# Source rows of an edge loop: gathered from memory, or made on chip by products of transposed one-hots

## The reference

```python
h = jnp.maximum(_layernorm(x, axis=-1), 0.0)
row, col = (edge_index[0], edge_index[1])
m = jnp.concatenate([x[row], x[col]], axis=1)
m = jax.nn.relu(m @ Wm1 + bm1)
m = jax.nn.relu(m @ Wm2 + bm2)
m_sum = jax.ops.segment_sum(m, row, num_segments=x.shape[0])
```

## Time and profile before

| | us |
|---|---|
| median of 3 runs (lowest, highest) | 1143.71 (1141.4, 1145.15) |
| profiled execution | 1144.47 |
| its span, first to last instruction | 1142.0 |
| TensorE busy | 841.2 (74%) |
| weight loads busy | 533.9 (47%) |
| VectorE busy | 661.6 (58%) |
| ScalarE busy | 461.4 (40%) |
| GpSimd busy | 368.7 (32%) |
| mean granted clock of TensorE | 0.914 of full |

### The profile page before, as it was taken

One profiled execution on the slowest core, in us unless ns is written; L12 is line 12 of the kernel. 1 busy time (PEld: TensorE's weight loads), 2 busy tenths in 40 slices (PEclk: granted clock), 3 DMA queues, 4 the chain that ended last, 5 costly groups with the idle time before them and its releaser, 6 DMA issues.

```text
span 1142.0 us, 17135 instructions
## 1 busy us (share of the span) xinstructions
PE 841.2 (74%) x5085; PEld 533.9 (47%) x5086; DVE 661.6 (58%) x1761; ACT 461.4 (40%) x956; POOL 368.7 (32%) x472
## 2 busy tenths in 40 slices
PE   4999627867787867677777768777687868776447
PEld 2568416756665756566666654531123213211243
DVE  6499924444444444444535446379848885996551
ACT  5321005434444444444435446534454444454200
POOL 7000265445554555545454550011301320212000
PEclk9999959888898899998989999889989999999778
DMA  2210132222222222222222340000000000000300
GB/s 70 88 44 1 33 97 64 65 78 69 87 72 80 73 92 70 77 74 73 83 73 83 73 91 1 1 0 1 1 1 0 1 1 1 0 1 0 148 1 19
DMA packets 26801, 53.84 MB, mean 47 GB/s; under 512 B 7440, under 2 KB 14736, under 8 KB 26768
## 3 DMA queue, kind: packets, MB, share of 16 engines
q0 software_dynamic: 14208, 38.82, 12.0%
q1 hardware_dynamic: 12560, 14.63, 3.9%
HBM read 46.60 MB, written 6.82 MB: 47 GB/s over the span
## 4 chain that ended last, share of the span: by engine, by line
PE 39%; DVE 19%; another core or an unknown queue 16%; ACT 12%; issue 9%; POOL 3%; ACTq 1%; DVEq 1%; DMA 0%; POOLq 0%
DVE OHd L853 8%; PE PS L989 6%; ACT OHe L470 5%; DVE PS L864 4%; PE PS L1089 3%; PE PS L1205 3%; PE PS L1131 2%; PE PS L1042 2%; PE PS L1196 2%; PE PS L1166 2%; PE PS L1086 2%; ACT OHs L472 2%; PE PS L1099 1%; PE PS L1107 1%
## 5 line engine op out<-in xcount | busy, mean ns | idle before, releaser
L364 POOL DMA_INDIRECT BT<-Ptab,gidx x148 | 143.2, 967 | 286.2 <-DVE MS L758 190.4
L470 ACT ACTIVATE OHe<-OHs,sew 128x128 bf16<-128x128 bf16 x408 | 126.9, 390 | 91.0 <-PE PS L1042 49.4
L364 POOL DMA_INDIRECT BT<-Qtab,gidx x148 | 143.1, 967 | 45.1 <-issue 45.1
L853 DVE CUSTOM_DVE_ANT_0 OHd<-PS,n1T 128x1024 bf16<-128x1024 f32 x96 | 113.4, 1219 | 15.7 <-PE PS L1166 15.7
L795 DVE TENSOR_SCALAR OHd<-iotaN,dstf 128x1024 bf16<-128x1024 f16 x136 | 64.5, 516 | 99.6 <-PE PS L1042 57.2
L1086 PE MATMUL PS<-OHd,OHc 128*128 x284 | 64.2, 226 | 69.0 <-ACT OHs L472 65.4
L758 DVE TENSOR_TENSOR MS<-BT 128x512 f32 x68 | 47.1, 692 | 113.7 <-remote 108.5
L393 POOL TENSOR_TENSOR zl<-AL,Sx 128x8 f32<-128x8 f32 x12 | 11.4, 947 | 291.0 <-DVE Sx L853 291.0
L1196 PE MATMUL PS<-rowA,sel 128*128 128x512 bf16 x192 | 61.5, 407 | 47.1 <-DVE PS L864 38.5
L1099 PE MATMUL PS<-OHs,m2s 128*128 128x128 f32 x544 | 89.6, 317 | 0.0
L1036 PE MATMUL PS<-Wm,m1T 128*128 128x256 f32 x272 | 85.7, 398 | 0.0
(11 more groups left out here) (326 smaller groups left out, 1663.3 us busy)
## 6 DMA issues: line engine op xcount, KB each, us to landing
BT<-Wtab SPq DMA_DIRECT2D x1, 4096.0 KB, 13.0
BT<-Ptab,gidx POOLq DMA_INDIRECT x148
BT<-Qtab,gidx POOLq DMA_INDIRECT x148
Wtab<-H SPq DMA_DIRECT2D x4, 512.0 KB, 2.7
Wtab<-cs SPq DMA_DIRECT2D x4, 512.0 KB, 3.2
Ptab<-BT SPq DMA_DIRECT2D x1, 1024.0 KB, 4.6
Qtab<-BT SPq DMA_DIRECT2D x1, 1024.0 KB, 7.1
Wn<-in_L_gnn_Wn SPq DMA_DIRECT2D x1, 1024.0 KB, 5.4
```

The costliest lines, as they stand in the source:

```text
L364: g.indirect_dma_start(out=G[:, p % SLOTS, t, k, :], out_offset=None, in_=tab, in_offset=bass.IndirectOffsetOnAxis(ap=gidx[:, p, 2 * t + k ...
L470: a.activation(OHe[:, k, j, :], OHs[:, k, :], ACT.Copy, scale=sew[:, j, bass.ds(2 * g + k, 1)])
L853: v.tensor_tensor_reduce(junk[n % 2], bank(4, 2), mask[:, i, :], 1.0, 2 * FAR, ALU.subtract, ALU.max, Sx[:, i, hd:hd + 1]).then_inc(S("gat ...
```

## The change

- The rows of P are no longer stored and gathered. GpSimd splits P into three bf16 parts (`Pp`, in the room of SKT, which is used later), L371 to L377 of the new file; the three add up to P. In the loop TensorE multiplies, for each chunk of a pair, a one-hot of the edge's source, transposed (nodes on partitions, edges on columns), with the three parts of the source block: six products of 256 columns into bank 5 (`sources`).
- The transposed one-hot is made by GpSimd (`turned`): it compares a row of source numbers, which stands on all partitions (`srow`), with the partition's number. The row comes from a transposition of `srcl` on TensorE, a copy to bytes on ScalarE, a store to memory (Stab) and two loads that spread it over all partitions: the first 8 pairs' part, then the rest.
- The message is bank 5 plus the gathered Q rows. A number for a pair's block is packed into the word that TensorE loads for each pair (`pblk`, `span`).
- The bias bm2 is added by VectorE from PSUM into m2s, and ScalarE's relu then works in place; the two bias products and the bf16 parts of bm2 go.
- The ranks move from bank 5 to the second half of bank 4, so five banks are cleared, and the rank products for the next pair now stand behind L1099 (L1175 of the new file). What waited for `pair_done` at a block's end waits for `ranks_done`. `counts_added` is told by the first product of the sums.
- The wait for the end of the gathers moves from b == 4 to b == 0 in the stage after the loop.

The core of the diff:

```diff
-        G = bflat[:, NB * N // 2:NB * N].rearrange("p (s t k f) -> p s t k f", s=SLOTS, t=2, k=2)
-        Ptab = nc.dram_tensor("Ptab", [N, F2], fp32, kind="Internal").ap()
+        G = bflat[:, NB * N * 3 // 4:NB * N].rearrange("p (s k f) -> p s k f", s=SLOTS, k=2)
+        srow = bflat[:, 0:NB * N * 3 // 4].bitcast(u8)[:, 0:NCH * P]
+        Pp = SKT[:].rearrange("p b n -> p (b n)")[:, 0:NB * 3 * F2].rearrange("p (b j f) -> p b j f", b=NB, j=3)
+        OHsT = KV[:].rearrange("p r k c -> p (r k c)").bitcast(bf16)[:, 0:SLOTS * PAIR]\
+            .rearrange("p (s e) -> p s e", s=SLOTS)
+        pid1 = sb("pid1", [P, 1])
+        srcT = sb("srcT", [P, 2, P], u8)
+        pblk = sb("pblk", [FEW, 2, NPAIR])
+        pblki = sb("pblki", [FEW, 1], i32)
+        Stab = nc.dram_tensor("Stab", [NCH, P], u8, kind="Internal").ap()
...
             eng.wait_ge(S("PQ_ready"), NB)
-            eng.dma_start(Ptab.rearrange("(b p) f -> p b f", p=P), PQ[:, :, 0, :]).then_inc(S("tables_stored"), 16)
             eng.dma_start(Qtab.rearrange("(b p) f -> p b f", p=P), PQ[:, :, 1, :]).then_inc(S("tables_stored"), 16)
-            eng.wait_ge(S("tables_stored"), 32)
+            eng.wait_ge(S("tables_stored"), 16)
...
+            eng.wait_ge(S("sources_across"), 1)
+            eng.dma_start(Stab[0:P, :], srcT[:, 0, :]).then_inc(S("sources_stored"), 16)
+            eng.dma_start(Stab[P:NCH, :], srcT[0:NCH - P, 1, :]).then_inc(S("sources_stored"), 16)
+            eng.wait_ge(S("sources_stored"), 32)
+            eng.wait_ge(S("P_parts"), 1)
+            flat = Stab.rearrange("c p -> (c p)")
+            eng.dma_start(srow[:, 0:SOON * PAIR], flat[0:SOON * PAIR].partition_broadcast(P))\
+               .then_inc(S("sources_soon"), 16)
+            eng.dma_start(srow[:, SOON * PAIR:], flat[SOON * PAIR:].partition_broadcast(P))\
+               .then_inc(S("sources_later"), 16)
...
-            eng.wait_ge(S("wm_loaded"), 64)
-            parts(bm2p[:], bm2[:])
-            g.sem_inc(S("bm2_parts"), 1)
...
+            eng.wait_ge(S("PQ_ready"), NB)
+            for j in range(3):
+                last = g.tensor_copy(Pp[:, :, j, :], PQ[:, :, 0, :])
+                if j < 2:
+                    split(last)
+                    split(g.tensor_tensor(PQ[:, :, 0, :], PQ[:, :, 0, :], Pp[:, :, j, :], ALU.subtract))
+            last.then_inc(S("P_parts"), 1)
+            split(g.tensor_scalar(pblk[:, 0, :], iota[0:FEW, 0:NPAIR], pb[0:FEW, 1:2], None, ALU.is_ge))
+            for b in range(2, NB):
+                split(g.tensor_scalar(pblk[:, 1, :], iota[0:FEW, 0:NPAIR], pb[0:FEW, b:b + 1], None, ALU.is_ge))
+                split(g.tensor_tensor(pblk[:, 0, :], pblk[:, 0, :], pblk[:, 1, :], ALU.add))
+            split(g.tensor_copy(pblki[:], pblk[:, 0, 1:2]))
+            g.tensor_scalar(pblk[:, 1, 0:NPAIR - 2], pblk[:, 0, 2:NPAIR], float(NB * NB), None, ALU.mult)
+            g.memset(pblk[:, 1, NPAIR - 2:NPAIR], 0.0).then_inc(S("pair_blocks"), 1)
+            eng.wait_ge(S("tables_stored"), 16)
+            eng.wait_ge(S("indices_ready"), 1)
             def gather(p):
                 if p >= SLOTS:
                     eng.wait_ge(S("msg_ready"), p - SLOTS + 1)
-                for t, tab in ((0, Ptab), (1, Qtab)):
-                    for k in range(2):
-                        g.indirect_dma_start(
-                            out=G[:, p % SLOTS, t, k, :], out_offset=None, in_=tab,
-                            in_offset=bass.IndirectOffsetOnAxis(ap=gidx[:, p, 2 * t + k:2 * t + k + 1], axis=0),
-                        ).then_inc(S(f"slot{p % SLOTS}_landed"), 16)
+                for k in range(2):
+                    g.indirect_dma_start(
+                        out=G[:, p % SLOTS, k, :], out_offset=None, in_=Qtab,
+                        in_offset=bass.IndirectOffsetOnAxis(ap=gidx[:, p, k:k + 1], axis=0),
+                    ).then_inc(S(f"slot{p % SLOTS}_landed"), 16)
+
+            def turned(p):
+
+                if p == 0:
+                    eng.wait_ge(S("sources_soon"), 16)
+                if p == SOON:
+                    eng.wait_ge(S("sources_later"), 16)
+                if p >= SLOTS:
+                    eng.wait_ge(S("msg_ready"), p - SLOTS + 1)
+                    eng.wait_ge(S("turned_onehots"), p - SLOTS + 1)
+                g.tensor_scalar(OHsT[:, p % SLOTS, :], srow[:, min(p, NPAIR - 1) * PAIR:][:, 0:PAIR], pid1[:], None, ALU.is_equal)\
+                    .then_inc(S("turned_onehots"), 1)
             def landed(p):
-                eng.wait_ge(S(f"slot{p % SLOTS}_landed"), 64 * (p // SLOTS + 1))
+                eng.wait_ge(S(f"slot{p % SLOTS}_landed"), 32 * (p // SLOTS + 1))
                 g.sem_inc(S("gathered"), 1)
             gather(0)
-            g.sem_inc(S("gathered"), 1)
-            for p in range(1, NASK):
+            gather(1)
+            turned(0)
+            turned(1)
+            landed(0)
+            for p in range(2, NASK):
+                turned(p)
                 gather(p)
                 landed(p - 1)
             landed(NASK - 1)
             g.sem_inc(S("gathers_over"), 1)
...
+            eng.wait_ge(S("sources_turned"), 1)
+            a.activation(srcT[:].rearrange("p c n -> p (c n)"), bank(7)[:, 0:2 * P], ACT.Copy, bias=1.0)\
+                .then_inc(S("sources_across"), 1)
...
-                    eng.wait_ge(S("m2_done"), g + 1)
-                    a.activation(m2s[:].rearrange("p k e -> p (k e)"), bank(7), ACT.Relu).then_inc(S("m2_ready"), 1)
+                    eng.wait_ge(S("m2_biased"), g + 1)
+                    a.activation(m2s[:], m2s[:], ACT.Relu).then_inc(S("m2_ready"), 1)
...
+            rankb = bank(4)[:, F2:2 * F2]
+
             def message(g):
                 slot = g & (SLOTS - 1)
-                eng.wait_ge(S("gathered"), g + 2)
+                eng.wait_ge(S("gathered"), g + 1)
                 eng.wait_ge(S("t_done"), g)
-                v.tensor_tensor(MS[:].rearrange("p k f -> p (k f)"),
-                                G[:, bass.ds(slot, 1), 0, :, :].rearrange("p o k f -> p (o k f)"),
-                                G[:, bass.ds(slot, 1), 1, :, :].rearrange("p o k f -> p (o k f)"),
+                eng.wait_ge(S("pparts_done"), g + 1)
+                v.tensor_tensor(MS[:].rearrange("p k f -> p (k f)"), bank(5),
+                                G[:, bass.ds(slot, 1), :, :].rearrange("p o k f -> p (o k f)"),
                                 ALU.add).then_inc(S("msg_ready"), 1)
...
+                    eng.wait_ge(S("m2_done"), g + 1)
+                    v.tensor_tensor(m2s[:], bank(7).rearrange("p (k f) -> p k f", k=2),
+                                    bm2[:].unsqueeze(1).to_broadcast([P, 2, F2]), ALU.add)\
+                        .then_inc(S("m2_biased"), 1)
                     message(g + 2)
...
-                if b == NB // 2:
+                if b == 0:
                     eng.wait_ge(S("gathers_over"), 1)
+                    eng.wait_ge(S("turned_onehots"), NASK)
...
-            for k in range(6):
+            eng.wait_ge(S("sources_ready"), 1)
+            t.matmul(bank(7), zeros[:, 0:P], zeros[:, 0:BANK], start=True, stop=True)
+            t.transpose(bank(7)[:, 0:P], srcl[:, 0:P], ident[:])
+            t.transpose(bank(7)[0:NCH - P, P:2 * P], srcl[:, P:NCH], ident[:]).then_inc(S("sources_turned"), 1)
+            for k in range(5):
...
                 to = bank(7)[:, k * F2:(k + 1) * F2]
-                t.matmul(to, sel3[:], bm2p[:], start=True, stop=False)
-                t.matmul(to, m1T[:, k, :], Wm2[:, 0, :], start=False, stop=False)
+                t.matmul(to, m1T[:, k, :], Wm2[:, 0, :], start=True, stop=False)
...
+            def sources(slot, blk):
+
+                for k in range(2):
+                    for j in range(3):
+                        last = t.matmul(bank(5)[:, k * F2:(k + 1) * F2],
+                                        OHsT[:, slot, k * P:(k + 1) * P], Pp[:, blk, j, :],
+                                        start=(j == 0), stop=(j == 2))
+                last.then_inc(S("pparts_done"), 1)
...
+            eng.wait_ge(S("turned_onehots"), 1)
+            sources(0, 0)
+            eng.wait_ge(S("pair_blocks"), 1)
+            second = eng.value_load(pblki[0:1, 0:1], min_val=0, max_val=NB - 1)
             eng.wait_ge(S("msg_ready"), 1)
-            eng.wait_ge(S("blocks_read"), 1)
             transposes()
+            eng.wait_ge(S("turned_onehots"), 2)
+            sources(1, second)
...
-                    span = eng.value_load(rngi[0:1, bass.ds(g, 1)], min_val=1, max_val=NB * NB - 1)
+                    span = eng.value_load(rngi[0:1, bass.ds(g, 1)], min_val=1, max_val=NB * NB * NB - 1)
+
+                    eng.wait_ge(S("turned_onehots"), g + 3)
+                    sources((g + 2) & (SLOTS - 1), (span >> 6) & (NB - 1))
                     eng.wait_ge(S("scaled_ready"), g + 1)
                     eng.wait_ge(S("counts_ready"), g + 1)
```

(11 more changed lines are left out.)

61 lines of the change are left out of this document (33 added, 28 removed).

## The result

| | before | after |
|---|---|---|
| median (lowest, highest) of 4 runs | 1142.56 us (1137.04, 1145.15) | 1045.62 us (1041.45, 1047.11) |
| span of the profiled execution | 1142.0 us | 1044.7 us |

The ratio is 0.915 (95% interval 0.911 to 0.920): 97 us less, where 49 were forecast. The time lies at the low edge of the range, on the number that rival B had (1047). The experiments will show that this ratio belongs to the place in which the two kernels ran: in others the same change makes the kernel 7.4% slower.

A forecast was written before the change was run, and what follows sets the result against it. It took the edge loop to be bound by a ring through GpSimd, whose gathers hold TensorE's signals. Sum: 1144.5 - 42 (loop) - 2 (block changes) - 14.5 (start) + 9 (sort) = 1095 us; range 1045 to 1138.

The forecast's parts named there:

- rival B: Edge loop: signals get through in time, TensorE bounds at 5.4 to 5.7 us a pair; 1047 us at 5.5; chance 0.22.
- What bounds the kernel before: Edge loop: TensorE's signals stand still while GpSimd issues gathers; 7.0 us a pair, TensorE busy in only 4.96.
- ring through GpSimd: Edge loop: message, gathers, release, message; new ring summed to 6.06 us, up to 6.94 with VectorE collisions.
- about 1.42 us for each gather: Time from first gather to release of TensorE's signals: 5.68 us for 4 gathers, 11.62 for 8, 39.34 for 28.
- The end of the hold of two gathers: Edge loop: TensorE's signals held from first gather to release, 2 x 1.42 = 2.84 us.
- I take 6.3: Edge loop: new period per pair 6.3 us, between 5.4 (TensorE) and 6.94 (VectorE collisions).
- 60 ordinary steps: Edge loop steps without a change of block: 60 x 0.7 = 42 us gained, ends 4 and 96.
- Sort: Sort phase: GpSimd's 16.6 us of making P's parts slows VectorE; 9 us lost, ends 3 and 16.6.
- Start: Start of the loop: first relu at 156.5 instead of 171.99, less 1 for transfers; 14.5 us gained, ends 5 and 18.
- Changes of block: Eight block changes: five banks cleared instead of six gains 3.7, later copies cost 1.4; net 2 us gained.
- After the loop: Stage behind the loop: the moved wait for the gathers' end is covered, or 1 us if not; 0 in the sum.
- Slower: Chance 0.12: most of a rival with nearly no gain, plus one whose hold lasts 5.68 us however few gathers.

The follow-up runs named there:

- e14: Kernel before, unchanged, in a free place (no signals held; kernel before takes about 968 us there): 965.2 us.
- e8: Separate test kernel, no part of the graph: TensorE signals beside trains of gathers, with and without comparisons between, in a holding place (kernel before about 1140 us); no total time given.
- e18: Kernel after with e7's edit and the six source products moved between the second layer's halves, holding place: 1034.1 us, ratio 0.902 to the kernel before.
- e6: Kernel after, unchanged, in a holding place: 1045.4 us.
- e5: Kernel before, unchanged, in a holding place: 1140.4 us.
- e13: Kernel after, unchanged, in a free place: 1038.6 us, ratio 1.074 to the kernel before.
- e7: Kernel after with GpSimd making P's parts block by block before the sort, holding place: 1029.9 us, ratio 0.903 to the kernel before.
- e9: Kernel before with only the two Q gathers per pair (P left out), same edit as e1, free place: 959.6 us, ratio 0.991.
- e1: Kernel before with only the two Q gathers per pair, the message adding the Q row to itself (P left out), free place: 961.6 us, ratio 0.993.

## Why the prediction was wrong

**What bounds the kernel before: right in a holding place.** Signals late by up to 3.8 us in an ordinary pair, a ring through GpSimd. What I could not see is that this is no property of the kernel: e14 has the same instructions and no late signal. I had written "so about 1.42 us for each gather" as if it were a cost of gathers. One profile can't tell that.

**The end of the hold of two gathers, 2.84 us: right.** In e8 it ends 2.9 us after the first of two gathers; in the kernel after, the rank products' update (end 447.98) came at 448.15, 2.77 after the first gather. But it begins late: in e8 updates up to 2.3 us after the first gather are on time. So two gathers mostly hold back what falls into the last 0.3 to 0.7 us of the 2.84; the latest update in the loop came 1.25 us late.

**"I take 6.3": the step that failed.** I put the whole 2.84 between GpSimd's gathers and the bias, as a link of a ring that sets the period, with `m2_done` "inside the hold". Measured, `m2_done` came 2.45 us after the first gather, as soon as TensorE was ready, so the ring is not closed by the hold: the loop's chain of waits is TensorE's alone and its step is 5.50 in a holding place as in a free one. The ring was also summed too long, which hid that it is the shorter of the two even with the hold in it: message to GpSimd 0.27 (measured 0.10, from 444.16 to 444.26), comparison 1.1 (0.94), gap 0.3 (0.17), bias, message and hand-overs 1.55 (0.04 + 0.69 + 0.69 = 1.42), and 0.24 on top for collisions (none to see: bias and message keep their 0.69, and VectorE's comparisons beside GpSimd's take 0.41 and 0.94, before 0.41 and 0.88). With the measured sizes it is 0.10 + 0.94 + 0.17 + 2.84 + 1.42 = 5.47, just under TensorE's 5.50. The 60 ordinary steps gave 83 us where 42 stood: 41 of the 49 us that the sum missed.

**Rival B had the mechanism, and its number in part by luck.** Signals get through in time and TensorE is the bound, as B said. But its 5.4 was TensorE's busy 4.96 less 0.22 plus 0.66. The true need before is 4.56 (e14), and 5.50 after is 0.94 more, not 0.44. The rest stands where L1166 begins: it starts 0.25 us behind the source products, and L1166 and L1169 take 1.12 us where L1086 and L1089 take 0.89. I put this down to the register steps that TensorE's sequencer does there; e18 shows that it goes when fp32 passes stand in between, but not that the registers are the reason.

**Sort: +9 forecast, +15.5 measured.** The first gather came 15.5 us later in the trace of the result, 14.2 in e6 against e5 and 13.8 in e13 against e14. I leaned to 70% and took 2.5 off for the ring of tiles. GpSimd's five large operations stood from 65.26 to 80.3, 15.0 us, and VectorE lost about all of it. The Trainium skill's rule (SBUF — State Buffer, "Who interferes with whom"), which I had set beside the sum, gave 16.6 by my price list; the trace and e7 agree with it for the large operations. That 16.6 lies near 15.5 is partly luck: my list had 13.6 for the large operations (15.0) and 3 for the small ones, which took 9.2 and cost VectorE little. And what stood still was mostly L727, which reads one tile, and not L728 with its two, of which I had quoted the rule. My own L659 rows were the weaker witness.

**Start, -14.5 against -18.3.** From first gather to first relu the kernel after takes 21.1 us, and 20.8 in the free place (e13). That is the 20.35 of TensorE's readiness at 153 and the bias 0.7: next to nothing is held there, where I had put 2.84, and nothing of the 1 us for the transfers shows.

**Changes of block, -2 against -6.0: right sign by another term.** The seven long steps contain an ordinary step each, which my sum left out and which alone saves 7 x 1.38 = 9.7 us. Above that they took 33.0 us before and 36.7 after, 32.4 and 32.9 in e5 and e6, so no gain from five banks shows.

**After the loop, 0 against -5.5.** This I can't place. Between e5 and e6 it was 2.4, in a free place nothing; three free traces whose code behind the loop is the same (e14, e9, e1) have 458.8, 461.6 and 464.4, so it lies within what the stage varies by.

**The chances.** Faster was right here. Slower, to which I gave 0.12 for other reasons, is what happens in the free places, mainly by a term that the prediction had as a gain: the loop.

## What to carry to other kernels

When a wait names no releaser and ends a fixed time after an engine's last gather, measure the kernel again elsewhere before paying for a cure: this one cost 71 us where there was nothing to cure. Where signals are held, part gathers in twos (shown in e8 alone, with a comparison of 0.95 us); where elementwise work of GpSimd must be done, put it beside an idle VectorE (13 to 15.5 us for a move of a few lines). Before a delay is put into a ring, ask when it begins as well as when it ends, and whether the signal that the ring needs falls inside. Sum the ring from gaps measured end to start, and hold it against the row of the busiest engine: 6.3 and 5.47 lie on two sides of 5.50.
